# Four layers of graph attention with residuals: order of VectorE in the second pass, a third bank for the output weights, and store waits behind the tables

## The reference

```
block 0: q, k = x Wq^T, x Wk^T; v = x Wv^T + bv; 12 heads of 32
         p = softmax(q k^T * 384^-0.5 + 2 adj), rows of zeros give 0;  p v Wo^T + bo
block 1: q, k, v = x W + b;  softmax(q k^T / sqrt(32) + beta adj, where adj > 0);  p v
block 2: two layers: a = softmax(h h^T / sqrt(384)); delta = a adj; attn = delta / (sum delta + 1e-10)
         ctx = upper(attn) (h Wl^T + bl) + diag(attn) (h Ws^T + bs) + lower(attn) (h Wr^T + br)
         h = relu(layernorm(ctx) * g + beta)
block 3: as block 0, with adj once
```

## Time and profile before

| | |
|---|---|
| median of 3 runs | 2617.66 us (2616.44 to 2620.24) |
| the profiled execution | 2617.5 us, span 2615.8 us |
| mean granted TensorE clock | 0.973 |
| busy: PE, PEld | 2438.8 us (93%), 2088.4 us (80%) |
| busy: DVE, ACT, POOL | 2003.8 us (77%), 1571.8 us (60%), 1969.0 us (75%) |

### The profile page before, as it was taken

One profiled execution on the slowest core, in us unless ns is written; L12 is line 12 of the kernel. 1 busy time (PEld: TensorE's weight loads), 2 busy tenths in 40 slices (PEclk: granted clock), 3 DMA queues, 4 the chain that ended last, 5 costly groups with the idle time before them and its releaser, 6 DMA issues. The chain is left out here.

```text
span 2615.8 us, 64634 instructions
## 1 busy us (share of the span) xinstructions
PE 2438.8 (93%) x21490; PEld 2088.4 (80%) x21490; DVE 2003.8 (77%) x3602; ACT 1571.8 (60%) x3348; POOL 1969.0 (75%) x2127
## 2 busy tenths in 40 slices
PE   6999999996999999959999998999997999999997
PEld 5888888885877777748888886888885888888886
DVE  4777878775788888877777776887884778777786
ACT  4667666674656656634545454656665667676664
POOL 4788878884677777765566566999995788888886
PEclk9999999997999999969999998999998999999998
DMA  8222222223433333315323316334343232332211
GB/s 139 63 71 70 68 70 67 68 58 69 90 78 79 79 76 79 80 57 113 72 64 73 67 53 130 99 95 107 99 99 82 57 72 61 70 73 68 58 53 46
DMA packets 320741, 200.90 MB, mean 77 GB/s; under 512 B 243440, under 2 KB 320624, under 8 KB 320624
## 3 DMA queue, kind: packets, MB, share of 16 engines
q1 hardware_dynamic: 317168, 198.12, 32.3%
q10 hardware_dynamic: 3456, 1.28, 0.3%
HBM read 136.42 MB, written 62.91 MB: 76 GB/s over the span
## 5 line engine op out<-in xcount | busy, mean ns | idle before, releaser
L487 PE MATMUL l_ps_p<-xT,w 128*128 128x512 f32 x2304 | 593.2, 403 | 55.6 <-DVE l_sc L815 14.4
L487 PEld LDWEIGHTS l_ps_p<-xT,w 128*128 128x128 f32 x2304 | 424.5, 191 | 151.2 <-issue 35.1
L1335 ACT ACTIVATE l_hlr<-l_ps_h 64x384 f32<-64x384 f32 x512 | 248.9, 486 | 313.1 <-PE l_ps_h L1260 304.4
L427 POOL TENSOR_TENSOR l_pr<-l_sc,l_st 128x768 f32<-128x768 f32 x192 | 286.5, 1492 | 173.3 <-DVE l_st L822 173.3
L832 DVE TENSOR_REDUCE l_st<-l_pr 128x12 f32<-128x768 f32 x192 | 182.8, 952 | 242.3 <-ACT l_pr L699 242.3
L381 POOL TENSOR_TENSOR v<-v,l_bvs 128x768 f32<-128x768 f32 x192 | 360.0, 1875 | 0.0
L1260 PE MATMUL l_ps_h<-second,xT 128*128 128x384 f32 x1728 | 323.7, 341 | 4.2 <-DVE l_hs L1463 4.0
L1185 POOL TENSOR_TENSOR l_hlr<-l_hlr,l_sides 128x768 f32<-128x768 f32 x128 | 235.7, 1842 | 121.2 <-ACT l_hlr L1335 114.6
L1260 PEld LDWEIGHTS l_ps_h<-second,xT 128*128 128x128 f32 x1728 | 298.6, 188 | 35.3 <-DVE l_hs L1463 17.4
L1260 PE MATMUL l_ps_h<-w,xT 128*128 128x384 f32 x1728 | 324.9, 342 | 0.0
L1260 PEld LDWEIGHTS l_ps_h<-w,xT 128*128 128x128 f32 x1728 | 299.7, 189 | 29.8 <-issue 27.5
(11 more groups left out here) (134 smaller groups left out, 4556.1 us busy)
## 6 DMA issues: line engine op xcount, KB each, us to landing
rows<-yo SPq DMA_DIRECT2D x256, 192.0 KB, 1.9
xa<-rows SPq DMA_DIRECT2D x256, 192.0 KB, 4.2
l_xr<-rows SPq DMA_DIRECT2D x192, 192.0 KB, 2.4
l_xr<-in_x SPq DMA_DIRECT2D x64, 192.0 KB, 2.5
out<-yo SPq DMA_DIRECT2D x64, 192.0 KB, 1.9
xa<-in_x SPq DMA_DIRECT2D x62, 192.0 KB, 4.2
l_edge<-in_adj SPq DMA_DIRECT2D x80, 128.0 KB, 2.3
raw<-in_L_gnn_Wk SPq DMA_DIRECT2D x12, 144.0 KB, 7.0
```

Source lines behind the costliest of these rows:

```text
L427: nc.gpsimd.tensor_tensor(pr[b][:, :, :], sc[b][:, :, :], st[b][:, 0, :].unsqueeze(2).to_broadcast([P, HEADS, NODES]), ALU.subtract).then_ ...
L487: last = nc.tensor.matmul(bank[:, :], W[m][:, l, t, o * P:(o + 1) * P], rows[:, r, t, :], start=c + t == 0, stop=c == 2 and t == KT - 1)
L1335: i = nc.scalar.activation(hlr[b][half * NODES:(half + 1) * NODES, g, :], ps_h[m][g * NODES:(g + 1) * NODES, :D], ACT.Copy)
```

## The change

Five edits. (1) SyncE's waits for the stores of the pass before stand behind the small tables, the edge table and the next pass's matrices (`attention_pass`), or behind the tables (`digcn_pass`). (2) The three transposed output weights have a bank each, with `ps_t` as third; TensorE waits for all three low parts before the first `probs_T`. (3) In the pass without output weights VectorE does `softmax_max(n)` before `residual(n-3)`. (4) In `digcn_pass` with `ends` the last unit uses `c1[b]` in place of `c3[b]` (`outer`), and ScalarE does its relu before the normed rows of unit 61. (5) GpSimd waits for the normed rows of unit 61 before the last outer norm.

```diff
@@ attention_pass, sync @@
-            for b in range(2):
-                if out_base:
-                    sp.wait_ge(s_out[b], out_base)
             if me.k == 0:
...
+            for b in range(2):
+                if out_base:
+                    sp.wait_ge(s_out[b], out_base)
             rows_in(2, 0)
@@ attention_pass, tensor @@
                 for t in range(KT):
-                    if t == 2:
-                        pe.wait_ge(dve_wo, 1)
                     for o in range(KT):
-                        last = nc.tensor.transpose((ps_o, ps_y)[t % 2][:, o * P:(o + 1) * P],
+                        last = nc.tensor.transpose((ps_o, ps_y, ps_t)[t][:, o * P:(o + 1) * P],
...
                 pe.wait_ge(pool_p if wo else act_e, n + 1)
+                if wo and isinstance(n, int) and n == 0:
+                    pe.wait_ge(dve_wo, KT)
@@ attention_pass, vector @@
-                    residual(n - 3, count, 1 - s % 2)
+                    if wo:
+                        residual(n - 3, count, 1 - s % 2)
                     softmax_max(n, par, s)
+                    if not wo:
+                        residual(n - 3, count, 1 - s % 2)
                     low_part(n - 2, s % 2)
@@ digcn_pass @@
+        def outer(n, b):
+            return c1[b] if isinstance(n, int) and n == units - 1 else c3[b]
...
             sp.dma_start(edge[0][:, :, :], adj_g[0]).then_inc(s_edge[0], 16)
-            for b in range(2):
-                sp.wait_ge(s_out[b], out_base)
...
             sp.dma_start(wt[1][:, :], ln_shift.to_broadcast([P, D])).then_inc(s_small, 16)
+            for b in range(2):
+                sp.wait_ge(s_out[b], out_base)
             rows_in(2, 0)
@@ digcn_pass, gpsimd @@
             outer_norm(units - 2, 0)
+            if ends:
+                pool.wait_ge(act_y, units - 2)
             outer_norm(units - 1, 1)
@@ digcn_pass, scalar @@
-                    if counted(n - 1):
+                    if counted(n - 1) and outer(n, b) is c3[b]:
                         act.wait_ge(act_y, n - 1)
...
             relu(units - 2, units // 2 - 1, 0)
+            relu(units - 1, units // 2 - 1, 1)
             normed(units - 3, units // 2 - 2, 1)
-            relu(units - 1, units // 2 - 1, 1)
```

More of the change, by code:

```diff
@@ L614, in output_weight_high @@
                 act.wait_ge(pe_wo, t + 1)
-                nc.scalar.activation(W[3][:, 0, t, :], (ps_o, ps_y)[t % 2][:, :D], ACT.Copy).then_inc(act_wo, 1)
+                nc.scalar.activation(W[3][:, 0, t, :], (ps_o, ps_y, ps_t)[t][:, :D], ACT.Copy).then_inc(act_wo, 1)
             def rows_high(g, gpar, t):
@@ L777, in output_weight_low @@
                 dve.wait_ge(act_wo, t + 1)
-                nc.vector.tensor_tensor(W[3][:, 1, t, :], (ps_o, ps_y)[t % 2][:, :D], W[3][:, 0, t, :].bitcast(F32),
+                nc.vector.tensor_tensor(W[3][:, 1, t, :], (ps_o, ps_y, ps_t)[t][:, :D], W[3][:, 0, t, :].bitcast(F32),
                                         ALU.subtract).then_inc(dve_wo, 1)
@@ L1167, in add_rows @@
                     pool.wait_ge(act_z, n + 1)
-                    nc.gpsimd.tensor_tensor(c3[b][:, :], c3[b][:, :], xr[b][:, :], ALU.add).then_inc(pool_res, 1)
+                    nc.gpsimd.tensor_tensor(outer(n, b)[:, :], outer(n, b)[:, :], xr[b][:, :], ALU.add).then_inc(pool_res, 1)
             def rows_low(g, gpar, tiles=range(KT)):
@@ L1343, in relu @@
                 if ends:
-                    if counted(n - 1):
+                    if counted(n - 1) and outer(n, b) is c3[b]:
                         act.wait_ge(act_y, n - 1)
-                    nc.scalar.activation(c3[b][:, :], c2[b][:, :], ACT.Relu).then_inc(act_z, 1)
+                    nc.scalar.activation(outer(n, b)[:, :], c2[b][:, :], ACT.Relu).then_inc(act_z, 1)
                 else:
@@ L1356, in normed @@
                         act.wait_ge(s_out[b], out_base + 16 * count)
-                    nc.scalar.activation(yo[b][:, :], c3[b][:, :], ACT.Identity, bias=ln[b][:, 21:22],
+                    nc.scalar.activation(yo[b][:, :], outer(n, b)[:, :], ACT.Identity, bias=ln[b][:, 21:22],
                                          scale=ln[b][:, 20:21]).then_inc(act_y, 1)
@@ L1496, in outer_stats @@
                 dve.wait_ge(pool_res, n + 1)
-                nc.vector.bn_stats(ln[b][:, 11:17], c3[b][:, :]).then_inc(dve_bn2, 1)
+                nc.vector.bn_stats(ln[b][:, 11:17], outer(n, b)[:, :]).then_inc(dve_bn2, 1)
                 dve.wait_ge(s_small, 16)
```

## The result

The changed kernel takes 2667.4 us (median of 4 runs, 2664.85 to 2669.18) against 2617.05 for the kernel before (4 runs, 2614.57 to 2620.24): ratio 1.0196, 95% interval 1.0183 to 1.0208. It is slower by 50 us, where 35.5 were forecast. The profiled execution has a span of 2667.2 us at a mean granted clock of 0.968.

What follows compares the result with a forecast made beforehand. The prediction took a ring through VectorE, GpSimd and ScalarE in the second pass as the bound. To 2617.5 us it added 38.7 - 1.4 - 0.3 - 1.5 = +35.5, giving 2653 us, range 2640 to 2676 (forecast alone 2646 to 2662).

Steps and rivals of the forecast that it cites:

- the ring: Second pass: maximum, statistics, L373, L375, L406 and subtraction come in one row; a group takes 34.04 us against 31.46.
- Intervals 0-1 and 2-3: Second pass, subtraction to subtraction, units 0 to 1 and 2 to 3: 8.31 and 8.36 us.
- 1-2: Second pass, subtraction to subtraction, unit 1 to 2: 10.29 us, with 2.50 for two L406 uncovered.
- Rival A: Second pass: the edit does what it says, statistics cost nothing, TensorE is the floor; 2601 us, chance 0.07.
- D: Second-pass loop bound by something the edit leaves alone, only the 3.2 us outside it move; 2614 us, chance 0.03.
- C: Second pass: L406 stays hidden behind VectorE's waits, 30 us rather than 38.7; 2642 to 2646 us, chance 0.14.
- Rival B: Second pass: TensorE's holes make its clock fall once a group, +15 to +30 us; 2668 to 2683 us, chance 0.14.
- 15 x 2.58 = 38.7 us: Second pass: fifteen groups go through the new order in full, each 2.58 us longer.
- The interval 3-0: Second pass, subtraction to subtraction, unit 3 to 0: 7.08 us, with no transposes or L406 added.
- The small savings: Outside the second-pass order: third bank -1.4, store waits -0.3, tail of the fourth pass -1.5 us.
- The third bank: Output weights, first and last pass: VectorE's 0.70 us of lateness saved twice, -1.4 us.
- The tail of the fourth pass: End of the fourth pass: GpSimd's last residual sum no longer waits for ScalarE's relu, -1.5 us.

Runs made afterwards that it cites:

- e1: The kernel before with only the new VectorE order in the second pass (maximum ahead of residual statistics): 2665.8 us, ratio 1.0187.
- e2: The changed kernel with the old VectorE order in the second pass, the other four edits kept: 2615.9 us, ratio 0.9998.
- e5: The changed kernel with GpSimd's L406 moved behind the subtraction L427 in the second pass, L373 staying ahead: 2633.1 us.
- e14: The changed kernel with only VectorE's normed rows L892 moved behind the row sum: 2710.9 us, ratio 1.0363.
- e11: The kernel before with only the third bank for the output weights: 2618.2 us, ratio 1.0008.
- e13: Changed kernel with old VectorE order, L400 ahead of L381, L406 and edge tables spread over later slots, and two output-weight banks: 2580.7 us, ratio 0.9863.
- e3: The changed kernel with GpSimd's L373 and L375 moved behind the subtraction L427 in the second pass, L406 staying ahead: 2658.7 us.
- e7: The changed kernel with L373, L375 and L406 behind the subtraction and L892 behind the row sum in the second pass: 2593.8 us, ratio 0.9918.
- e8: The changed kernel with the old VectorE order and GpSimd's L400 ahead of L381 in the second pass: 2585.7 us, ratio 0.9889.

## Why the prediction was right, and where it was off

**The mechanism** stands: the ring through VectorE's maximum and statistics, GpSimd's L373 and L406, and the subtraction. Intervals 0-1 and 2-3 were forecast within 0.1 us. That 1-2 came to the hundredth is in part luck: two L406 took 2.60 us instead of 2.50, and the transposes and the maximum 0.12 less. The total of 2667.4 is above the 2646 to 2662 that the forecast gave to this mechanism; it lies in the stated range only because that was drawn wider for the rivals. Rival A (the edit does what it says) falls with the waits of L373, D with e1 and e2, C with the intervals of 10.29 and 8.43 and with e5 (its own terms give 2642 to 2644, not 2646). Rival B, the clock, falls too, near as 2667 is to its 2668: 0.99 was granted in the stretch, with two falls to 0.50, at 716 us for 6.8 us and at 784 for 3.4, and these groups took no longer (34.25 and 34.73 us) than the others. No single wait of TensorE there is longer than 1.3 us. In e14 the clock fell once a group from 865 us on, and the group of 37.39 us did not change by it.

**The mis-sized term** is "15 x 2.58 = 38.7 us". It measured 49.9:

- 14 groups at 3.07 instead of 2.58 us: +6.9. The interval 3-0 was "7.08" and is 7.31. From 892.72 on, subtraction to row sum takes 2.50 us instead of 2.39 (this subtraction is 1.59 long, the one in the forecast 1.48), row sum to scores' read 1.24 instead of 1.15, statistics to L373 0.91 instead of 0.88. In every second group it is 7.72: VectorE's L815 stands 0.4 us with nothing to wait for (the "issue" row above), at the place where the kernel's loop over pairs of groups starts over. Before, that stood inside L880's wait for L400; now it is in the ring.
- The last group: +4.5 instead of 2.6 us. VectorE and GpSimd there do work for the next pass's weights in their slots as well; how the 1.9 divides was not taken apart.
- Group 0, left out of the forecast as it has statistics in its last slot only: +1.4; the pass's head and end +1.0.

**The small savings**, "-3.2", measured about nothing (e2: -0.02% with an interval of 0.1% to either side). Each of the three shows in the trace, none in the time.

The third bank did remove TensorE's 1.88 us of waiting. VectorE's low parts now follow each other and the scores' read comes at once (after, VectorE in the first pass, against the earlier trace rows):

```profile
40.04 0.55 DVE L778 TENSOR_TENSOR w<-l_ps_t,w 128x384 fp32r<-128x384 f32 x1
40.50 0.95 DVE L815 SCALAR_TENSOR_TENSOR l_sc<-l_ps_s,l_sbias 128x768 f32<-128x768 f32 x1
```

The first subtraction was 1.38 us ahead of before. Of that, 0.59 is not the bank's: TensorE began these transposes at 37.02 instead of 37.61. Counted from there, the first subtraction comes after 5.57 us here, and after 5.56 to 5.61 in all ten traces with three banks, against 6.36 or 6.89 in the four with two. So the bank gives at least 0.79, near the 0.70 of the forecast. But TensorE had done its work earlier too and stood longer for the first probabilities, and here the clock stayed low for longer, against the earlier trace rows:

```profile
48.00 1.54 PE L521 MATMUL l_ps_t<-ident,l_pr 128*128 128x128 f32 x6 [3.34 <-POOL l_pr L436]
```

```profile
50.00:51.00 1.00, 1.00 (x3) 0.75 (x3) 0.32 (x1) 0.02 (x1) 1.00 (x2) 0.50 0.00 0
51.00:52.00 1.00, 1.00 (x4) 0.76 (x3) 0.00 (x0) 0.00 (x0) 1.00 (x2) 0.50 0.00 0
52.00:53.00 1.00, 1.00 (x4) 0.81 (x3) 0.00 (x0) 0.00 (x0) 0.79 (x1) 0.50 0.00 0
53.00:54.00 1.00, 1.00 (x4) 0.76 (x4) 0.00 (x0) 0.58 (x2) 0.00 (x0) 0.61 0.00 0
```

and the same microsecond before (TensorE alone):

```profile
53.00:54.00 1.00, 1.00 (x6) 0.83 0.00 0
```

By the third subtraction the gain is gone: 23.19 us after those transposes, against 23.14 before. None of it reaches e11's time. The length of the hole does not decide what the clock does. All ten traces with three banks have a hole of 3.3 us there. After it the clock was at 0.50 for 6.8 us in five of them (the third subtraction 23.2 us after the transposes), for 3.4 us in two (22.1 to 22.2) and not at all in three (20.7 to 20.8). Before, and in e13, both with two banks, it was at 0.50 for 3.4 us (23.1 and 23.0). So this point differs by up to 2.4 us with the clock, three times what the bank gives. What decides between the three courses no run here shows.

The tail of the fourth pass is 1.4 us shorter, by the time from the last context product's end to the next pass's first instruction (11.98 us instead of 13.39), against 1.5 forecast; it is 10.8 to 12.3 in the eleven traces with this edit, 13.2 to 13.4 in the three without. The residual sum no longer waits for the relu, only 0.20 us for its rows:

```profile
2050.21 0.99 POOL L1176 TENSOR_TENSOR l_c<-l_c,l_xr 128x384 f32<-128x384 f32 x1 [0.20 <-DMA l_xr<-rows]
```

The store waits did what was forecast at the queue: in the third pass the issue behind the edge load follows it by 0.44 us instead of 0.53. No run has this edit alone.

The second pass starts between 635.4 and 641.3 us over all fourteen kernels, which differ in the first pass by the third bank at most, with no order by edit. The +2.0 here is of that kind, and as large as all the small edits together. It arises at the pass's end: from the last subtraction to the next pass's first instruction it is 23.7 us against 21.3 before, and 23.7 in e13 as well, which has two banks.

**Not foreseen**: that the length of VectorE's normed rows depends on what GpSimd does meanwhile. It made e3 miss upward and e7 downward. The forecast itself did not hang on it, as their length hardly changed (1422 to 1460 ns).

## What to carry to other kernels

When the producer of a semaphore moves later on one in-order engine, look at where its consumer stands on the other: all that is queued behind that wait moves with it, and what was hidden beside the old position is now in series (here 3.1 us in a group, of which 2.0 go when L406 moves, which had nothing to do with the statistics). The wait that showed in the trace, statistics for L400, was better removed from its own side, by issuing L400 one instruction earlier: 30 us faster instead of 50 slower, though nearly half of that came from an operation that grew shorter beside it. Sum the ring in instructions, and look at rows with "issue" before them on its engines: what was slack before the change can be on the path after it.

## What the runs showed of the hardware

VectorE's normed rows (a tensor_scalar of 128x384 from SBUF to SBUF) are short alone and long beside GpSimd. The kernel before shows both, in its loop and at the pass's end:

```profile
885.33 1.47 DVE L892 TENSOR_SCALAR yo<-l_res,l_ln 128x384 f32<-128x384 f32 x1
...
1165.31 0.48 DVE L892 TENSOR_SCALAR yo<-l_res,l_ln 128x384 f32<-128x384 f32 x1 [1.50 <-POOL l_ln L375]
```

The long ones end some 0.2 us after the GpSimd operation beside them: 886.80 where the subtraction ends at 886.59, and in e7 893.49 where L381 ends at 893.28 (891.44 + 1.84). One of 0.50 us in e7 (883.61) ends 0.22 us after the L406 that was running when it began. So an operation of this kind lasted until some 0.2 us after the GpSimd operation in flight ended, and 0.48 us when there was none. The first edge table goes from 1.56 us to 0.61 and the second from 1.94 to 0.48 in e7, where only the first 0.5 us lie beside the subtraction; in the earlier trace rows both lay beside it and L381, and in e8, beside L400, the second took 1.11. Row sum, maximum and statistics (0.95, 0.95, 0.55) do not lengthen beside GpSimd in the timelines read here.

The Trainium skill (SBUF — State Buffer, SBUF: two separate sides) says that VectorE and GpSimd share a pair of ports as an exclusive lock held for a whole instruction, taken by VectorE in a 2-port mode or with two SBUF inputs (against a GpSimd operation that reads SBUF, as those here do). The trace agrees in kind: the normed rows and both edge tables (the second has two SBUF inputs) do not end before the GpSimd operation beside them. In size it agrees less. By a full wait the normed rows would need their own 0.48 us after the other's end, and they end 0.2 us after it; the ends of GpSimd's operations are rough in a profile, so this may be theirs. That the lengthened ones run in such a mode no run here shows, and no run changed only what lies beside an operation.
